# Attention stack on one core: softmax sums inverted in compact form, one block of rows for the maxima of both head halves, and order lists of their own for each layer

## The reference

```python
# layers 0, 1 and 3: attention with 8 heads of 32 features
scores = q @ k.T / sqrt(32)           # layer 0: masked where adj and eye are 0
                                      # layer 1: + a_i + c_j + b_g + log(adj + 1e-9)
                                      # layer 3: + log(clip(adj, 1e-8))
out = softmax(scores) @ v
# layer 0 and 3: layernorm(x + out @ Wo.T + bo) * gamma + beta;  layer 1: x + out
# layer 2: graph attention
fp = x @ W_fc + b_fc
z = (fp @ w_q + b_q) + (fp @ w_k + b_k).T + (1 - adj) * -1e9
out = softmax(leaky_relu(z, 0.01)) @ fp + x
```

## Time and profile before

| | |
|---|---|
| median of 3 runs | 2000.71 us (1999.82 to 2002.35) |
| the profiled execution, its own time | 1996.07 us |
| its span, first to last instruction | 1993.8 us |
| mean granted PE clock | 0.969 |
| busy: PE, DVE, POOL, ACT | 91%, 83%, 62%, 61% |
| PE weight loads | 68% |

### The profile page before, as it was taken

One profiled execution on the slowest core, in us unless ns is written; L12 is line 12 of the kernel. 1 busy time (PEld: TensorE's weight loads), 2 busy tenths in 40 slices (PEclk: granted clock), 3 DMA queues, 4 the chain that ended last, 5 costly groups with the idle time before them and its releaser, 6 DMA issues.

```text
span 1993.8 us, 54761 instructions
## 1 busy us (share of the span) xinstructions
PE 1805.7 (91%) x23693; PEld 1359.4 (68%) x23756; DVE 1659.6 (83%) x2656; ACT 1223.2 (61%) x1894; POOL 1235.7 (62%) x730
## 2 busy tenths in 40 slices
PE   5899998899999999889999999988999999987996
PEld 4666775677667677567766677657776677756774
DVE  4899887668899988767889989776889998877687
ACT  2566754457766675356766676535776677644575
POOL 3442776278954487527984458734896536872678
PEclk7999998999999999999999999999999999989998
DMA  5110010101220000000121000010021100001000
GB/s 148 34 33 12 18 34 12 33 12 44 65 61 27 12 18 28 22 22 18 60 65 54 13 17 18 23 43 7 28 65 54 44 18 18 19 21 38 12 28 33
DMA packets 67730, 66.44 MB, mean 33 GB/s; under 512 B 6050, under 2 KB 67492, under 8 KB 67492
## 3 DMA queue, kind: packets, MB, share of 16 engines
q1 hardware_dynamic: 67492, 62.95, 10.3%
HBM read 54.54 MB, written 8.39 MB: 32 GB/s over the span
## 4 chain that ended last, share of the span: by engine, by line
PE 54%; DVE 30%; ACT 9%; issue 4%; POOL 1%; SPq 1%; DMA 0%; DVEq 0%; POOLq 0%; ACTq 0%
PE gx L530 18%; PE sc L629 12%; PE od L664 11%; DVE rden L920 6%; DVE ring L915 5%; DVE qk L860 3%; PE gx L677 3%; DVE negm L881 3%; ACT aside L761 2%; ACT ring L776 2%; DVE negm L878 2%; PE gx L644 2%; PE sc L635 2%; PE sc L623 1%; DVE lg L954 1%
## 5 line engine op out<-in xcount | busy, mean ns | idle before, releaser
L515 POOL TENSOR_TENSOR ring<-ring,adj_c 128x1024 f32<-128x1024 f32 x256 | 608.6, 2403 | 157.5 <-ACT ring L774 90.3
L629 PE MATMUL sc<-qk 32*128 32x256 f32 x9216 | 418.2, 298 | 41.9 <-ACT aside L761 15.1
L629 PEld LDWEIGHTS sc<-qk 32*128 32x128 f32 x9216 | 330.4, 188 | 174.3 <-issue 137.7
L920 DVE RECIPROCAL rden<-od 128x256 f32<-128x256 f32 x192 | 335.7, 1748 | 6.3 <-PE od L664 6.3
L776 ACT ACTIVATE ring<-sc 128x1024 f32<-128x1024 f32 x256 | 248.5, 1024 | 67.3 <-PE sc L635 66.6
L520 POOL TENSOR_TENSOR xs<-xs,lr_g 128x512 f32<-128x512 f32 x64 | 82.7, 1293 | 322.4 <-ACT xs L783 322.4
L881 DVE TENSOR_REDUCE negm<-aside 128x4 f32<-128x1024 f32 x192 | 233.2, 1215 | 47.5 <-ACT aside L761 47.5
L878 DVE TENSOR_REDUCE negm<-sc 128x4 f32<-128x1024 f32 x192 | 234.1, 1219 | 33.3 <-PE sc L629 17.9
L664 PE MATMUL od<-ring,vf 128*32 128x256 f32 x3072 | 251.4, 400 | 1.3 <-POOL ring L515 1.3
L664 PE MATMUL od<-ring,ones_r 128*32 128x256 f32 x3072 | 240.6, 386 | 0.0
L761 ACT ACTIVATE aside<-sc 128x1024 f32<-128x1024 f32 x192 | 195.8, 1020 | 56.4 <-PE sc L635 28.5
(11 more groups left out here) (139 smaller groups left out, 4332.9 us busy)
## 6 DMA issues: line engine op xcount, KB each, us to landing
adj_c<-in_adj_t SPq DMA_DIRECT2D x96, 256.0 KB, 2.8
adj_r<-in_adj SPq DMA_DIRECT2D x64, 256.0 KB, 3.1
xs<-in_x SPq DMA_DIRECT2D x32, 256.0 KB, 2.8
out<-xs SPq DMA_DIRECT2D x32, 256.0 KB, 2.1
ring<-in_w_q SPq DMA_DIRECT2D x2, 256.0 KB, 5.7
ring<-in_w_k SPq DMA_DIRECT2D x2, 256.0 KB, 6.0
wo<-in_w_o SPq DMA_DIRECT2D x2, 256.0 KB
ring<-in_w_v SPq DMA_DIRECT2D x1, 256.0 KB, 3.8
```

Source lines behind the costliest of these rows:

```text
L515: pool.tensor_tensor(part, part, adj_c[i.mi % 3][:, t, :].unsqueeze(1).to_broadcast([P, G, N]), ALU.mult).then_inc(weighted, 1)
L629: mm = pe.matmul(sc[:, g, t * N:(t + 1) * N], buf[rows, a, c, t * P:(t + 1) * P], buf[rows, b, c, :], start=(n == 0 and not masked), stop= ...
L920: dve.reciprocal(rden[grp][:], od[grp][:, N:2 * N]).then_inc(rden_set, 1)
```

## The change

1. N: the reciprocal of 128x256 gives way to three DVE instructions: a transpose by blocks of 32x32, which leaves each sum once in every block column, a reciprocal of 8 columns, and a transpose back that reads each of the 8 columns 32 times.
2. U and M: the maxima of both head halves share one `negp` of two blocks in place of four. PE makes two matmuls in place of four, ACT copies 128x256 in place of 128x512, and E adds the rows with a stationary `pick` that has ones at two of four rows, one pair for each half. In layer 1 the subtraction and addition of the gate stand in one instruction. POOL sets `pick` at the start with 13 memsets.
3. Layer 2: J writes its diagonal into the first half of `lg` in place of a `dk` of its own, and five `fp` buffers stand in place of four, so one rule of order between K and G is gone.
4. The tables of places: one for each layer, with new numbers throughout; new places for stage I, where the bias fold's spreading stands with weight 3 in place of 2. `GAT_START`, `LAST_START` and the form of `PITCH` are new as well, and the order of the items stays the same.
5. The identity is made in a corner of `ring`, and DVE's copy of it is the one that all use.

```diff
-NFP = 4
+NFP = 5
...
-MHA_PLAN = {
-    "T": {PE: [-0.473], ACTE: [-0.446], DVE: [-0.471]},
...
+MHA_PLAN0 = {
+    "T": {PE: [-1.369], ACTE: [-0.812], DVE: [-0.531]},
...
-            at.append((max(n - 4, -1) + 0.95, 0, n, engine, "I", items[0]))
+            at.append((-0.05 if n < 3 else 1.55 + (n - 3), 0, n, engine, "I", items[0]))
...
+            flat_pick = pick[:].bitcast(F32)
+            pool.memset(flat_pick, 0.0).then_inc(pick_set, 1)
+            n = 1
+            for rows, h, value in ((2, 0, 1.0), (4, 1, 1.0), (2, 1, 0.0)):
+                for g in range(G):
+                    pool.wait_ge(pick_set, n)
+                    pool.memset(flat_pick[DH * g:DH * g + rows, h, :], value).then_inc(pick_set, 1)
+                    n += 1
...
+            pe.wait_ge(ident_set, 1)
             for s, i, c in order[PE]:
...
-                    extra = m_rows[i.mi % 2][:, c, :] if s == "E" else c_rows[i.i1 % 2][:] if i.l == 1 else None
+                    if s == "E":
+                        extra, spread, depth = m_rows[i.mi % 2][:], pick[:, c, :], 4
+                    else:
+                        extra, spread, depth = c_rows[i.i1 % 2][:] if i.l == 1 else None, ones_r[:], 2
...
-                    for n in range(C * T):
+                    for n in range(T):
                         mm = pe.matmul(gx_of("m", i)[:, n * P:(n + 1) * P], negp[i.mi % 2][:, n, :], ident_r[:],
...
-                    act.activation(m_rows[i.mi % 2][:].rearrange("p c n -> p (c n)"), gx_of("m", i)[:], ACT.Copy)\
+                    act.activation(m_rows[i.mi % 2][:], gx_of("m", i)[:, 0:N], ACT.Copy)\
...
-                        act.activation(dk[i.gi % 2][:, t, :], ident[:], ACT.Copy, scale=fp[i.gi % NFP][:, t, D + 1:D + 2])\
+                        act.activation(lg[i.gi % NLG][:, t * P:(t + 1) * P], ident, ACT.Copy, scale=fp[i.gi % NFP][:, t, D + 1:D + 2])\
...
-                    if c == 2:
+                    if c == 3:
                         dve.wait_ge(w_plain, 16 * len(plain))
...
-                            dve.tensor_scalar(neg[:, :, t, :], neg[:, :, t, :], a[:, t:t + 1], None, ALU.subtract).then_inc(shifted, 1)
+                            dve.tensor_scalar(neg[:, :, t, :], neg[:, :, t, :], a[:, t:t + 1], a[:, t:t + 1], ALU.subtract, ALU.add)\
+                                .then_inc(shifted, 1)
...
+                    dve.tensor_copy(pad[:, :, :, :, 0], neg[:]).then_inc(neg_hi_set, 1)
+                    dve.wait_ge(neg_hi_set, i.mi + 1)
+                    dve.tensor_tensor(pad[:, :, :, :, 1], neg[:], pad[:, :, :, :, 0].bitcast(F32), ALU.subtract).then_inc(negp_set, 1)
...
-                    dve.reciprocal(rden[grp][:], od[grp][:, N:2 * N]).then_inc(rden_set, 1)
+                    dve.transpose(rden[grp][:], od[grp][:, N:2 * N]).then_inc(turned, 1)
+                    dve.wait_ge(turned, C * i.mi + grp + 1)
+                    dve.reciprocal(rden8[grp][:], rden[grp][:, 0:N:DH]).then_inc(inverted, 1)
+                    dve.wait_ge(inverted, C * i.mi + grp + 1)
+                    dve.transpose(rden[grp][:], rden8[grp][:].unsqueeze(2).to_broadcast([P, N // DH, DH])).then_inc(rden_set, 1)
```

More of the change, by code:

```diff
@@ new lines @@
+MHA_PLAN3 = {
+    "T": {PE: [-1.19], ACTE: [-1.073], DVE: [-0.698]},
+    "Q": {PE: [0.636], ACTE: [0.369], DVE: [1.202]},
+    "P": {PE: [1.218], ACTE: [1.533], DVE: [2.181]},
+    "V": {PE: [5.67], ACTE: [6.124], DVE: [-9.553]},
+    "S": {PE: [3.514, 5.371], ACTE: [4.002, 5.553], DVE: [4.205, 5.767]},
+    "U": {DVE: [6.406]},
+    "M": {PE: [7.81], ACTE: [8.254]},
+    "E": {PE: [8.642, 10.048], ACTE: [8.758, 10.82], POOL: [7.379, 7.824], DVE: [4.208, 7.121]},
+    "A": {PE: [11.495, 12.869, 14.21, 14.607]},
+    "N": {DVE: [13.302, 15.208]},
+    "F": {PE: [19.244]},
+    "XB": {POOL: [-1.681]},
+    "H": {DVE: [19.215]},
+    "LC": {SP: [1.4]},
+    "PC": {POOL: [0.247]},
+}
@@ L64 @@
+LN_PLAN0 = {
+    "B": {DVE: [20.521]},
+    "Z": {ACTE: [21.887]},
+    "Y": {DVE: [27.099], ACTE: [28.749], POOL: [28.572]},
+}
+LN_PLAN3 = {
+    "B": {DVE: [19.777]},
+    "Z": {ACTE: [22.008]},
+    "Y": {DVE: [23.028], ACTE: [25.306], POOL: [23.757]},
 }
 FIRST_PLAN = {
-    "LX": {SP: [-6.376]},
-    "LR": {SP: [-4.102]},
-    "PR": {POOL: [-3.153]},
+    "LX": {SP: [-5.633]},
+    "LR": {SP: [-11.454]},
+    "PR": {POOL: [-3.015]},
 }
@@ L73 @@
 GAT_PLAN = {
[L74 to L83, removed]
[L84 to L86 removed]
+    "T": {PE: [-1.283], ACTE: [-1.168], DVE: [-0.48]},
+    "G": {PE: [0.327, 0.617], DVE: [0.68, 0.921]},
+    "J": {ACTE: [1.277]},
+    "K": {PE: [6.757]},
+    "L": {DVE: [7.376]},
+    "X": {ACTE: [8.099]},
+    "W": {PE: [11.782], ACTE: [11.913]},
+    "C": {DVE: [13.038], PE: [12.846]},
+    "LR": {SP: [11.922]},
+    "PR": {POOL: [0.713]},
+}
+PITCH = {0: (4, 4), 1: (4, 4), 2: (4.5, 4.5), 3: (4, 4)}
+GAT_START, LAST_START = 24, 33.5
 class Item:
@@ L118, in all_items @@
         i.place(k, start, items[:k])
-        start += PITCH[i.l]
+        start += PITCH[i.l][i.slot % 2]
     return items
@@ L217, in gnn_stack @@
             in_order(("C", gats[n - NLG].k, 0), ("K", i.k, 0))
-        if n >= 2:
-            in_order(("K", gats[n - 2].k, 0), ("G", i.k, T - 1))
+            assert order[ACTE].index(("W", gats[n - NLG], 0)) < order[ACTE].index(("J", i, 0))
+    for engine in (PE, ACTE, DVE, POOL):
+        for group in ("T", "QP", "V", "S", "U", "M", "E", "A", "N", "F", "H", "B", "Z", "Y", "G", "J", "K", "L", "X", "W", "C", "XB", "PR", "PC"):
+            stages = (group,) if len(group) > 1 and group != "QP" else tuple(group)
+            run = [(i.k, stages.index(s), c) for s, i, c in order[engine] if s in stages]
+            assert run == sorted(run), (engine, group)
     with ExitStack() as ctx:
```

112 lines of the change are left out of this document (58 added, 54 removed).

## The result

The changed kernel takes 1915.55 us (median of 4 runs, 1908.63 to 1919.46) against 2001.13 us (4 runs) of the kernel before: ratio 0.9569, 95% interval [0.954, 0.9598]. I had forecast 1874 with a range of 1835 to 1925. So it is faster by 86 us where I expected 127, and the time lies outside the 1842 to 1906 that I gave for the forecast itself. The profiled execution took 1908.63 us, 7 us under its median, with a span of 1906.8.

A forecast was written before the change was run, and what follows sets the result against it. It took PE as the bound, DVE close behind. Terms summed to 32.9 us a group (484.5 to 451.6); four groups, 55.8 us start and end and 5 us lost led to 1874 us, own range 1842 to 1906, stated 1835 to 1925.

The forecast's parts named there:

- The bound: Whole kernel: PE leads, busy 91% of the span, with DVE near at 83%, so little of DVE's saving becomes time.
- rival (b): New lists trade old waits between layers for new ones, gaining nothing there or from the clock: 1933 us; chance 0.15.
- M: Adding the maxima on PE: two fewer matmuls save 0.25 us an item on the path, 24 us in all.
- settled slots: Time between same stage of two successive items: 5.2, 4.4, 6.6 and 2.0 us a group saved, layers 0 to 3.
- the seams: Where layers overlap: half of PE's other 25 us of idle time goes, 12.7 us a group saved.
- N: Compact inversion on DVE: 1.0 us in place of 1.75, saving 0.75 us a head half, 144 us of DVE.
- Rival (c): Transposes are slow, 1.75 us each, and DVE becomes the bound: about 2135 us; chance 0.03.
- the 0.42 us wait: Layer 0: PE idles 0.42 us a slot until DVE's residual sum empties a `gx` bank; this was to go.
- The circle I named: Layer 2: waits through `xt_lo` and the same item's exponential; new order brings 5.4 us, saving 6.6 us a group.
- the clock: PE's granted clock: fewer pauses give back 2 us of the 9.5 us a group lost.
- The start: Program start: first graph's load issued later, first scores near 43 us, 5 us lost (3 won to 10 lost).
- DVE's busy time: DVE over the whole run: busy near 1500 us, named as a sign that the forecast holds.

The follow-up runs named there:

- Experiment 1: The kernel before with only the compact inversion (three DVE instructions for the full reciprocal), old lists and old rows of maxima: 1976.83 us, ratio 0.9906.
- experiment 3: The changed kernel with the old tables of places, stage I and bias fold as before, all other code new: 1939.76 us, ratio 0.9715.
- experiment 5: The changed kernel with POOL's product of layer 1 on 8 of 256 columns, leaving out most of the adjacency weighting there: 1839.74 us, ratio 0.9199.
- experiment 6: The changed kernel without the gate's arithmetic in U of layer 1, which cancels but for rounding: 1890.03 us, ratio 0.9448.
- experiment 7: The changed kernel without the gate's arithmetic, and with U's copy and subtraction done by three reduces: 1864.32 us, ratio 0.9321.
- Experiment 4: The changed kernel with SP issuing the first graph's loads first again, ahead of the small vectors: 1917.68 us, ratio 0.9594.
- experiment 11: The changed kernel with U by reduces, no gate arithmetic, and the first graph's loads issued first: 1855.07 us, ratio 0.9298.

## Why the prediction was right or wrong

**The bound: right.** PE leads, and filled slots are PE's. The sign held. That the stated range held is in part luck: 1915.6 is outside the range of the forecast, and inside the stated one because that took in a part of rival (b). In the sum itself M and the settled slots gave more than I had put there, and the seams far less.

**N: right in size, wrong in its use.** Transposes take 0.442 and 0.445 us where I took 0.42. The small reciprocal takes 0.204, not 0.155: an inversion is 1.09 us and saves 0.65 instead of 0.75. Rival (c), slow transposes, is out. DVE in layer 0's slot came to 16.34, near the forecast 16.3, though an item's two inversions save 1.3 us and not 1.5. Three instructions in place of one were no step back. But I gave the 0.42 us wait two reasons, DVE's room and the new order. Experiment 1 has the room without the order, and the wait stands.

**Settled slots: 21.8 us a group, forecast 18.2.** Layer 0 gave 8 x 0.8 = 6.4 (5.2), layer 1 8 x 0.95 = 7.6 (4.4), layer 3 8 x 0.6 = 4.8 (2.0), layer 2 only 6 x 0.5 = 3.0 (6.6). This takes one slot times eight, as the forecast did. By whole stretches the layers 0 to 3 gained 7.5, 3.1, 5.3 and 8.1 us: in layer 1 less than half of what its settled slot promises.

**M: too small.** I counted 24 us by the start spacing of two matmuls; the step from experiment 1 to 3 is 38. It holds M, ACT's shorter copy (0.378 us where it was 0.598), which I had counted at nothing although E waits for it, and the smaller edits. Which of them brings the rest was not tried apart. Nor did the 0.25 us come where I put it: from experiment 1 to 3 the settled stretch from M to M goes from 18.29 to 18.31 us in layer 0, from 16.35 to 16.24 in layer 1 and from 16.05 to 15.61 in layer 3.

**Layer 2: mis-sized.** The circle I named is gone, and another stands at 6.0 us, not 5.4:

```profile
819.43 0.63 PE L767 MATMUL gx<-ident_r,lg 128*128 128x128 f32 x4 [0.16 <-DVE fp L1004]
820.42 0.63 PE L614 MATMUL gx<-ident_r,xs 128*128 128x128 f32 x4 [0.37 <-DVE lg L1013]
823.84 0.39 PE L589 MATMUL gx<-wh_fc,xt_hi 128*128 128x258 f32 x1 [0.31 <-DVE xs L1031]
```

These rows of the timeline show three waits, each for a `gx` bank that DVE has to empty. I followed the data (the exponential, `xt_lo`), not the banks.

**The seams and the clock: the step that failed.** I took half of 25 us plus 2 for the clock, 14.7 us a group. The group gained 24.0, of which the slots hold 21.8: the seams and clock gave 2.2. The waits behind stretched DVE instructions are 12.0 us a group; 2.2 + 12.0 is nearly the 14.7. So the lists did end old waits, and a new one took their place, one that no list shows: DVE standing still behind POOL. Experiments 5 to 7 show the mechanism. The stretches from one M of layer 1 to the next show what it costs, here three of the changed kernel and two of experiment 7 at the same places:

```profile
712.38:730.47 18.09, 15.40 (x249) 12.14 (x245) 16.15 (x25) 11.55 (x18) 17.50 (x11) 1.00 0.06 17
730.47:748.00 17.53, 16.90 (x244) 13.40 (x244) 12.78 (x27) 9.73 (x16) 11.49 (x8) 0.90 0.06 17
763.33:781.01 17.68, 10.71 (x187) 7.51 (x183) 15.71 (x21) 7.63 (x10) 16.50 (x9) 0.97 0.01 2
...
706.61:721.92 15.31, 15.31 (x248) 12.09 (x244) 11.90 (x25) 10.52 (x17) 14.74 (x10) 1.00 0.07 19
752.57:764.10 11.53, 10.63 (x187) 7.48 (x183) 9.42 (x19) 7.62 (x10) 11.37 (x7) 1.00 0.01 3
```

The wait of 2.69 us makes 18.09 us out of 15.31. Behind it PE is granted a clock of 0.90, and the next stretch takes 17.53 us where experiment 7 has 15.32 at a clock of 1.00. The wait of 6.07 us makes 17.68 out of 11.53. Together 11.1 us a group, and the stretch behind them, to layer 3's first M, takes 70.6 us instead of 72.2. The stay at the first seam remains (3.26 us, and 3.69 in experiment 7); the clock of the stretch around it is 0.92 in the changed kernel and 0.80 in experiment 7, and that stretch takes 2.7 us longer there, though one group of experiment 7 has it at 0.92 as well. In all a group of experiment 7 takes 450.1 us, 10.4 less, and near the 451.6 of my sum. Four groups are 42 us; the ratios give 50 and the two profiled spans 40, all with the gate's arithmetic left out.

This is rival (b) in kind, a new wait for an old one. I had let it come from the places in the lists alone and gave it 0.15.

**The start: right at its own point, and more around it.** The first S came at 42.85 us, forecast near 43. But start and end together grew from 55.8 to 64.8 us, 9 where I had 5. Experiment 4 shows that the order of the first loads does not mend it alone. In experiments 4 and 11 the early loads bring the first M 4.9 and 5.1 us forward, which is the size that I had forecast; in the time only experiment 11 has it, and not clear of the noise. Where the other 4 us of start and end went was not tried.

**DVE's busy time: 1550.6, forecast 1500.** It is 1659.6 less 126 for the inversions, plus 27 of stretching (94.2 - 67.6), less some 10 for U's and other small changes. A busy time above the sum of the parts was the sign on the page.

## What to carry to other kernels

Look at least, median and most of small DVE instructions in the trace of before. A tail that ends with a POOL instruction says that their time depends on when they run, and a change of order or of durations can then cost more than it saves, without any instruction getting slower in itself. What stands on a critical path beside a busy POOL was better written here as a reduce, even with one instruction more. Transposes and operations that read PSUM did not stretch either, but were not tried in its place. A gain of one part should be measured with the others in and out: the same inversion was worth 19, 106 and 16 us in three settings.

## What was not expected of the hardware

A DVE instruction on 16 columns that takes 0.18 us took up to 2.36 us beside a POOL product, and in the rows above the ends of such instructions fell within 0.05 us of the end of POOL's. In the changed kernel 63 instructions of U take over 0.1 us more than their median, and 57 of them end within 0.06 us of the end of a POOL instruction. The `tensor_reduce` of the same 16 columns stayed at 0.169 to 0.192 us in 288 instances. A DVE transpose of 128x256 in float32 takes 0.44 us both out of PSUM and from SBUF with each element read 32 times, as long as a multiplication of that size (0.424); the reciprocal of 8 columns takes 0.204 and that of 256 columns 1.748 us. The clock granted behind one and the same wait differs from group to group and from run to run (0.79 or 0.92 at the seam from layer 0 to 1 in experiment 7, 0.82 or 0.90 behind the wait of 2.69 us in experiment 4 and the changed kernel), which is worth 1.5 to 3 us each time.
